# Six layer norms: four tiles' roots taken a stage earlier, turnings tile by tile, 20 unread products ahead of them

## The reference

```python
def _layernorm(x, axis=-1, eps=1e-05):
    m = jnp.mean(x, axis=axis, keepdims=True)
    v = jnp.var(x, axis=axis, keepdims=True)
    return (x - m) / jnp.sqrt(v + eps)

x = x + 0.5 * L0_ffn(_layernorm(x), ...)   # stage 0: dense 512x512 and a low-rank part mixed by 8 soft experts
x = x + L0_attn(_layernorm(x), ...)        # stage 1: causal attention, 32 heads of 16, with 10 adapter keys
x = x + 0.5 * L0_ffn(_layernorm(x), ...)   # stage 2: as stage 0
x = x + 0.5 * L1_ffn(_layernorm(x), ...)   # stage 3: 16 experts, the best 2 of each token, and a shared one
x = x + L1_attn(_layernorm(x), ...)        # stage 4: grouped attention, 32 heads of 128 on 8 keys, no mask
x = x + 0.5 * L1_ffn(_layernorm(x), ...)   # stage 5: as stage 3
```

## Time and profile before

| | |
|---|---|
| median of 3 runs | 1725.32 us (1724.57 to 1725.44) |
| profiled execution, its own time | 1734.16 us |
| its span | 1732.3 us |
| mean granted TensorE clock | 0.97 of full speed |
| busy: TensorE, VectorE, ScalarE, GpSimd | 93%, 58%, 53%, 57% of the span |
| norm instructions of the six stages (L168) start at | 11.0, 64.0, 425.8, 478.7, 677.0, 1534.3 us |

### The profile page before, as it was taken

How to read it: one execution, slowest core, us unless ns; L and a number is a source line. 1 busy time by engine, 2 the same in 40 slices (tenths; PEclk the granted TensorE clock), 3 DMA queues, 4 the chain that set the end, 5 groups by cost and what they waited for, 6 DMA issues and landing times. The chain is left out here.

```text
span 1732.3 us, 26681 instructions
## 1 busy us (share of the span) xinstructions
PE 1603.9 (93%) x8364; PEld 1248.4 (72%) x8364; DVE 1001.3 (58%) x2614; ACT 914.6 (53%) x1881; POOL 990.0 (57%) x1156
## 2 busy tenths in 40 slices
PE   6899999998979996889999999999999999979998
PEld 4587565656667874678878787877878788767886
DVE  6651656644583237465665666666675756666235
ACT  2212767661232222677777777777777777731231
POOL 2342646530313632688777788778787787812533
PEclk9899989998989998999999999999999999989999
DMA  2200000001076643445344443534445344454934
GB/s 88 104 1 3 2 1 2 2 2 38 1 271 220 226 151 115 91 104 122 86 110 111 107 115 79 124 94 109 121 100 131 73 104 91 92 184 161 344 126 152
DMA packets 311297, 179.99 MB, mean 104 GB/s; under 512 B 281608, under 2 KB 282968, under 8 KB 308769
## 3 DMA queue, kind: packets, MB, share of 16 engines
q1 hardware_dynamic: 299360, 152.54, 31.4%
q0 software_dynamic: 11840, 26.25, 4.8%
HBM read 111.08 MB, written 22.54 MB: 77 GB/s over the span
## 5 line engine op out<-in xcount | busy, mean ns | idle before, releaser
L1381 POOL TENSOR_TENSOR st_prob<-st_prob,st_rinv 128x512 f32<-128x512 f32 x256 | 273.7, 1069 | 167.4 <-DVE st_rinv L1463 167.4
L1385 POOL TENSOR_TENSOR st_plane<-st_prob,st_plane 128x512 f16<-128x512 f32 x256 | 311.1, 1226 | 0.2
L1470 DVE TENSOR_REDUCE st_nmax<-st_score 128x1 f32<-128x512 f32 x256 | 175.3, 685 | 198.1 <-PE st_score L114 197.6
L1316 ACT ACTIVATE st_prob<-st_score,st_nmax 128x512 f32<-128x512 f32 x256 | 175.3, 685 | 82.2 <-DVE st_nmax L1470 80.3
L1300 ACT ACTIVATE st_plane<-st_prob 128x512 f16<-128x512 f32 x256 | 160.3, 626 | 108.1 <-POOL st_prob L1381 107.9
L1426 DVE CAST st_ptlo<-st_plane_t 128x512 fp32r<-128x512 f16 x256 | 175.2, 685 | 2.4 <-DMA st_plane_t<-st_plane 2.4
L1295 ACT ACTIVATE st_pthi<-st_plane_t 128x512 fp32r<-128x512 f16 x256 | 159.7, 624 | 6.8 <-DMA st_plane_t<-st_plane 6.6
L2143 DVE CUSTOM_DVE_ANT_0 st1b_dump<-st1b_score,st1b_maskrow 128x128 f32<-128x128 f32 (+3 forms) x256 | 112.8, 488 | 82.2 <-PE st1b_score L1796 56.5
L791 POOL DMA_INDIRECT st_xg<-rows,st_source x62 | 62.8, 1013 | 108.3 <-DVE st_source L979 61.3
L1992 ACT ACTIVATE st1b_slabs<-st1b_across 128x512 f32<-128x512 f32 (+1 forms) x192 | 91.1, 531 | 61.0 <-PE st1b_across L1818 45.8
L661 PE MATMUL st_bank<-st_xts,st_raw 128*128 128x128 f32 x992 | 121.0, 275 | 0.7 <-issue 0.7
(11 more groups left out here) (395 smaller groups left out, 4001.4 us busy)
## 6 DMA issues: line engine op xcount, KB each, us to landing
st_raw<-in_moe_w SPq DMA_DIRECT2D x40, 768.0 KB, 17.8
sorted_outs<-st_ln_xn SPq DMA_DIRECT2D x62, 256.0 KB
st_qraw<-in_gqa_q SPq DMA_DIRECT2D x8, 1024.0 KB, 5.2
st_oraw<-in_gqa_o SPq DMA_DIRECT2D x8, 1024.0 KB, 5.2
rows<-st_ln_xn SPq DMA_DIRECT2D x2, 2048.0 KB, 14.7
st_kvraw<-in_gqa_kv SPq DMA_DIRECT2D x8, 512.0 KB, 3.9
st_plane_t<-st_plane SPq DMA_TRANSPOSE x256
st1a_raw<-in_w_attn SPq DMA_DIRECT2D x3, 1024.0 KB, 5.5
```

The lines of the kernel that those rows point to most:

```text
L1316: act.activation(prob[:, t, :], score[t][:, :], ACT.Exp, bias=nmax[:, slot:slot + 1], accum_out=rsum[:, slot:slot + 1]).then_inc(exp_ready, 1)
L1381: pool.tensor_tensor(prob[:, t, :], prob[:, t, :], rinv[:, slot:slot + 1].broadcast_to([P, T]), ALU.mult).then_inc(norm_ready, 1)
L1385: pool.tensor_tensor(plane[t][:, T:2 * T], prob[:, t, :], plane[t][:, 0:T], ALU.subtract).then_inc(lower_ready, 1)
L1470: dve.tensor_reduce(nmax[:, slot:slot + 1], score[t][:, :], AX, ALU.max, negate=True).then_inc(nmax_ready, 1)
```

## The change

- `Moments.early` on VectorE, once the statistics of four tiles are there (tiles 0 to 3): aggregation of these four, variance plus epsilon, a wait for ScalarE's root (`early_root`), and the chain of five (`inverse_root`). It stands in the stage that makes x; in stage 0's entry it stands between the fourth and the fifth tile's statistics. `close` aggregates only tiles 4 to 7.
- `vector_rows` then issues the variance of the late four tiles, the rows of the first four, and behind them the wait for the late root, the late chain and four rows.
- The turnings go tile by tile: TensorE waits for one row and turns its four blocks into four banks, so that the four banks of a half are complete with the fourth tile's turnings.
- Ahead of the turnings of each norm stand 20 products of the identity by itself, into the last bank of the norm.
- In stages 0 and 2 the statistics of the seventh tile and `early` stand ahead of the last add. In stage 3 the statistics of tiles 0 to 3 and `early` stand ahead of the four last adds. In stage 4 ScalarE's `root_table` and `early_root` stand ahead of `out_hi`.
- The small buffers of the roots are shared by all stages.

```diff
+def inverse_root(dve, root, cols, step, done):
+    ve, ra, rb, rc = (root[n][:, cols] for n in ("ve", "ra", "rb", "rc"))
+    dve.reciprocal(ra, root["sd"][:, cols]).then_inc(step, 1)
+    dve.wait_ge(step, done + 1)
+    dve.tensor_tensor(rb, ra, ra, ALU.mult).then_inc(step, 1)
+    dve.wait_ge(step, done + 2)
+    dve.tensor_tensor(rc, rb, ve, ALU.mult).then_inc(step, 1)
+    dve.wait_ge(step, done + 3)
+    dve.tensor_scalar(rb, rc, -0.5, 1.5, ALU.mult, ALU.add).then_inc(step, 1)
+    dve.wait_ge(step, done + 4)
+    dve.tensor_tensor(rc, ra, rb, ALU.mult).then_inc(step, 1)
+    dve.wait_ge(step, done + 5)
...
 class Moments:
...
+    def early(self, dve, taken):
+        half = slice(0, TB)
+        dve.wait_ge(self.stats_ready, taken)
+        for t in range(TB):
+            dve.bn_aggr(self.mv[:, t, :], self.stats[:, t, :]).then_inc(self.mv_step, 1)
+        dve.wait_ge(self.mv_step, TB)
+        dve.tensor_scalar(self.root["ve"][:, half], self.mv[:, half, 1], 1e-5, None, ALU.add).then_inc(self.mv_step, 1)
+        dve.wait_ge(self.early_std, 1)
+        inverse_root(dve, self.root, half, self.mv_step, TB + 1)
+
+    def early_root(self, act):
+        act.wait_ge(self.mv_step, TB + 1)
+        act.activation(self.root["sd"][:, 0:TB], self.root["ve"][:, 0:TB], ACT.Sqrt).then_inc(self.early_std, 1)
+
+    def close(self, dve, rest):
         dve.wait_ge(self.stats_ready, NT)
-        for t in range(NT):
-            dve.bn_aggr(self.mv[:, t, :], self.stats[:, t, :]).then_inc(self.mv_ready, 1)
-        dve.wait_ge(self.mv_ready, NT)
+        for t in rest:
+            dve.bn_aggr(self.mv[:, t, :], self.stats[:, t, :]).then_inc(self.mv_step, 1)
+        dve.wait_ge(self.mv_step, NT + 6)
...
 class Norm:
...
     def vector_rows(self, dve):
+        late = slice(self.early, NT)
+        def row(t):
+            dve.tensor_scalar(self.rows[t], self.x[:, t, :], self.mv[:, t, 0:1], self.root["rc"][:, t:t + 1],
+                              ALU.subtract, ALU.mult).then_inc(self.xn_ready, 1)
+        dve.tensor_scalar(self.root["ve"][:, late], self.mv[:, late, 1], 1e-5, None, ALU.add).then_inc(self.var_ready, 1)
+        for t in range(self.early):
+            row(t)
         dve.wait_ge(self.std_ready, 1)
...
+        inverse_root(dve, self.root, late, self.rstd_step, 0)
+        for t in range(self.early, NT):
+            row(t)
...
     def tensor(self, pe):
-        for n, (h, k) in enumerate(self.order):
-            pe.wait_ge(self.xn_ready, TB * (h + 1))
+        warm(pe, self.bank[-1], self.ident, 20)
+        for h in range(B):
             for t in range(TB):
-                last = pe.transpose(self.bank[n][:, t * P:(t + 1) * P], self.rows[h * TB + t][:, k * P:(k + 1) * P], self.ident[:, :])
-            last.then_inc(self.turned_ready, 1)
+                pe.wait_ge(self.xn_ready, TB * h + t + 1)
+                for k in range(KC):
+                    last = pe.transpose(self.bank[h * KC + k][:, t * P:(t + 1) * P], self.rows[h * TB + t][:, k * P:(k + 1) * P], self.ident[:, :])
+                    if t == TB - 1:
+                        last.then_inc(self.turned_ready, 1)
...
# stage 0, ScalarE
                     entry.root_table(act)
+                    entry.early_root(act)
                 norm.scalar_std(act)
...
# stage 0, VectorE
                         entry.take(dve, t)
-                    entry.close(dve)
+                        if t == TB - 1:
+                            entry.early(dve, TB)
+                    entry.close(dve, range(TB, NT))
...
# stages 0 and 2, VectorE, ahead of the adds
                 for j in range(NT):
+                    if j == NT - 1:
+                        dve.wait_ge(x_added, j)
+                        moments.take(dve, order[j - 1])
+                        moments.early(dve, j)
                     dve.wait_ge(tile_ready, j + 1)
...
-                    if j >= 1:
+                    if 1 <= j < NT - 1:
...
# stages 3 and 5, VectorE
-                for t in range(TB):
-                    add_step(NI - 1, 1)
+                if not last_stage:
+                    for t in range(TB):
+                        wait(dve, *written[t])
+                        moments.take(dve, t)
+                    moments.early(dve, TB)
+                add_step(NI - 1, 1)
+                for t in range(TB, NT):
+                    if t + 1 < NT:
+                        add_step(NI - 1, 1)
                     if not last_stage:
                         wait(dve, *written[t])
                         moments.take(dve, t)
...
# stage 4, ScalarE
                     turned_hi(LAST, NU - 1, t)
+                moments.root_table(act)
+                moments.early_root(act)
                 out_hi(LAST, NU - 1)
-                moments.root_table(act)
...
# stages 1 and 4, VectorE, behind the statistics of tiles 0 to 3
+                moments.early(dve, TB)
```

More of the change, by code:

```diff
@@ L1018, in _ @@
                 if not last_stage:
[L1019 to L1022 removed]
+                    moments.close(dve, range(TB, NT))
 def gqa_stage(nc, env, dram, name):
```

50 lines of the change are left out of this document (20 added, 30 removed).

## The result

| | before | after |
|---|---|---|
| time, median of 8 runs (lowest to highest) | 1725.32 us (1714.22 to 1728.27) | 1736.09 us (1734.81 to 1746.19) |
| ratio, with its 95% interval | | 1.0081 (1.0057 to 1.0105) |
| the profiled execution: time, span | 1734.16, 1732.3 us | 1746.19, 1744.5 us |
| TensorE busy, records | 1603.9 us, 8364 | 1629.8 us, 8604 |
| mean granted clock | 0.970 | 0.975 |

The change makes the kernel 0.8% slower, 14 us by the ratio; the two medians lie 10.8 us apart. More runs on another chip gave 1.0074 (1.0053 to 1.0096). The forecast was 7.8 us slower. The sign was right, the size was about half of the ratio's; the measured 1736.1 lies inside the range given, 3 us above the point.

The account below looks back on a forecast made before the run. TensorE, busy 93%, bounds the kernel, so only moves of each norm's gate (a stage's first product waiting for four xlo) and of stage ends count; terms sum to +7.8 us, forecast 1733.1, range 1726.5 to 1739.

Parts of the forecast that it names:

- stage 2: Second FFN stage's norm: products begin where turnings stood, less 0.3 us each for start and rows; gate +2.3 us.
- rival 2: All norms: fast clock comes 6.4 us after the start, products take 7.5 us; some +14 us, 1739; chance 0.10.
- The price of 20 products: Head of each norm: 40 records, partly at 1.2 GHz, together 6.8 us.
- Rival 3: All norms: an identity product takes one pass, head 4.3 us; sum +1.2 us, 1726.5; chance 0.03.
- rival 1: All norms: products meet or quickly make 2.4 GHz, 4.6 us instead of 6.8; sum -0.4, 1724.9; chance 0.13.
- Stage 0: Entry norm: a VectorE row held by GpSimd's wlo, gate +3.1 us, 0.9 back from the clock; +2.2 us.
- Rival 4: Stage 0: VectorE isn't held, roots pay; last row at 20; with rival 1 some -4 us, 1721.5; chance 0.06.
- Stage 1: Heads stage's norm: gate waits for GpSimd's wlo, -0.2 us, and warmer clock behind it gives 1.3; -1.5 us.
- End of the first expert stage: Last adds wait behind four statistics and the early part; +0.6 or, at low clock, +3.1 us; taken as +2.1.
- Stage 3: First expert stage's norm: gate 11.45 us after TensorE's start, at 489.9 instead of 488.19; +1.7 us.
- Stages 4 and 5: Norms of grouped attention and last stage: 11.45 us from start to gate; +0.6 and +0.4 us.
- The first bank: Each norm: first bank is full only with the fourth tile's first turning, 13 records, 1.45 us.

Follow-up runs that it names:

- forty products: Changed kernel with 40 identity products at each norm in place of 20; ratio 1.0266 to the kernel before.
- old entry and tail: Changed kernel with one root for eight tiles in stage 0 and the first expert stage's last adds in front, as before; ratio 1.0086 to the kernel before.
- bank by bank: Changed kernel with the turnings ordered as before, four of one bank and then the next bank; ratio 1.0068 to the kernel before.
- all but the products undone: Changed kernel with old stage 0 and expert-end orders, turnings by bank, 40 filling instructions; products and other early roots stay; ratio 1.0043 to the kernel before.
- no products: Changed kernel without the 20 products at each norm, all else kept; ratio 1.0054 to the kernel before.

## Why the prediction was right in sign and half in size

Two steps failed. One is in the sum: "TensorE reaches the products where the turnings stood, less 0.3 each" gave stage 2 +2.3 us, and it measured +4.3, because the chain that lets TensorE go on had not moved. The other is a term that the prediction put at nothing: "Behind it TensorE runs nearly without gaps, so I price each norm by how far its gate moves". Behind the gate of the grouped attention five instructions more in ScalarE's program made five stalls, 3.6 us. The rest of the difference is sizes. That the time lies inside the range is partly luck, since the range's upper end belongs to rival 2, and 7.5 us of products at every norm is not what came.

The terms of the sum, in its order, against what the two profiles of the changed kernel show beside those of the kernel before:

- **The price of 20 products.** Right. 40 records each, 6.97, 6.33, 7.23, 6.41, 7.54 and 6.72 us; their mean is 6.87, the forecast had 6.8. (One record is 0.117 us at 2.4 GHz, by forty against twenty, not 0.115; the row read for it, 2.47 us for 20 records, holds the end of the last one too.) They have one spread from stage to stage, as the low clock takes more or less of each. Rival 3 (one pass) and rival 1 (4.6 us) are out for these two profiles, and so is rival 2's 7.5 everywhere.
- **Stage 0**, +2.2: gate +3.2 and +2.7 in the two profiles (forecast +3.1), and 1.2 us back behind it from the clock (0.9): +1.7. The held row is the mechanism that was named; wlo began at 17.35, not 17.5. Rival 4 is out. With the old entry the gate was at 24.7, so the early root costs 1.5 of it.
- **Stage 1**, -1.5: -1.7, of which 0.1 at the gate and 1.6 behind it, where no matmul was slow.
- **Stage 2**, +2.3: +4.4 and +4.5 at the gate, less 0.15 behind it: +4.3. The step that failed is "TensorE reaches the products where the turnings stood, less 0.3 each". What TensorE waited for there was neither rows nor the stage's start but the chain load, low-rank product, aw copy (the row says so: the head waits 0.28 us for `st_aw`), and that chain had not moved. And the clock was low until 439.2, not for 3 us of the head: 7.23 us and not 6.0. By the terms: start 0.6, head 1.2, turning to copy 0.2.
- **End of the first expert stage**, +2.1: +3.1 and +3.0. The mechanism and both ends of the range were right, and it was the end with the low clock; I had rounded a three in four down. Against all seventeen profiles it is +2.5, nearer to the forecast.
- **Stage 3**, +1.7: +1.6.
- **Stages 4 and 5**, +0.6 and +0.4: +1.3 and +0.7 against the first profile, but against six more executions in which these norms were as before (11.2 to 11.8, mean 11.4, and 11.2 to 12.2, mean 11.6, from end to gate) more like +2.2 and +1.4. The profile on which the sum was made had late gates there by itself; I took one execution's 10.83 for the price of the stage. The head of stage 4 was 7.54 us.
- **The first bank**, 1.45 us in the sum, took 1.62 us every time. Small, but bank by bank it takes 0.64; that tile by tile costs 1 us at each gate behind products was inside the sum and nowhere named.
- **Not in the sum at all**: the stalls of ScalarE's loop in the attention, 3.6 us at +5 instructions without the change, and what the same body lost with it (851.9 and 850.8 against 845.2 and 848.1, 847.4 with the loop moved on by 40). I had priced every instruction that ScalarE got, in place, and none by where it puts those behind it.

Taken together: +1.7 - 1.7 + 4.3 + 3.05 + 1.6 + 1.3 + 0.7 + 3.6 = +14.6 us, beside 14 (9.8 to 18.1) measured. The forecast's 7.8, the 3.6 of the stalls, 2.0 more in stage 2, 0.95 at the expert end and 1.0 in stages 4 and 5, less 0.8 in stages 0, 1 and 3, are the same sum. With the terms from more executions (2.5 at the expert end, 2.2 and 1.4 in stages 4 and 5) it is 15.6. So the agreement to half a microsecond is luck, that within the interval isn't. The spans of the two first profiles themselves differ by 12.2 us, and chance is in that too: the first expert stage took 173.8 us from its gate to the last combining against 177.7 before, and the last stage 181.7 from its gate against 187.3; in the second pair of profiles these were 177.3 against 177.0 and 188.3 against 185.8. What makes them so was not looked for. The full price of twenty products is read from forty against twenty, 28 us; the first twenty cost less, since a part of them stood beside rows, loads and splits.

What stays open: the rest of the attention's difference. In three profiles (the changed kernel twice, and with 40 instructions of filling) TensorE lost 1.4 to 1.7 us more at a wait for a pthi copy some 130 us behind the gate; in the other fourteen, forty products among them, it did not. And three ratios (old entry and tail, all but the products, no products) are 3 to 8 us above what the gates, ends and stalls of their traces give.

## What to carry to other kernels

Work put in front of a gate to warm a clock is paid in full unless a named wait at that gate ends later than the work does: here one gate of six had such a wait (a GpSimd split behind a load), and there it gave back 1.6 us in the trace, which the time didn't show (0.9994). When an edit lengthens an engine's program ahead of a loop, compare the idle time "issue" and the count of instruction packets inside that loop before and after; a loop of 279 instructions began to be fetched anew at each jump back when it lay 2 to 18 instructions further on, and at 30 and more it had stopped. Price an order of "statistics first, adds second" by who waits for the adds, and take a stage's base from more than one execution.

## What the runs showed of the hardware that was not expected

- ScalarE stalls 1.4 to 2.7 us at a jump back in a band of positions of its loop: bad at 2, 4, 5 and 18 instructions from the kernel before, good at 0, 30, 44 and 45, with five more 8 KB packets a pass where it stalls. Seven profiles with five stalls lost 2.6 to 3.7 us by them.
- The low clock of the heads stage differs between executions of one kernel (24 and 31 us before, 31 and 21 after), and it moves that stage by more than any term of the change: the same 2240 matmuls took 343.6 to 355.3 us. These are the windows from gate to end for the kernel before and for all but the products undone (PE busy, PEld, DVE, ACT, POOL, then the clock, DMA share and GB/s):

```profile
76.08:425.28 349.20, 333.06 (x2240) 227.28 (x2240) 184.97 (x664) 172.55 (x347) 156.75 (x413) 0.97 0.02 8
```

```profile
74.76:418.37 343.61, 327.69 (x2240) 223.28 (x2240) 186.56 (x671) 173.21 (x348) 156.25 (x413) 0.99 0.02 8
```

- A row of VectorE stood through a GpSimd subtraction whenever rows were left when it began (6.08 us for four rows here, 8.24 for eight with the old entry). One execution, of the kernel before with 30 idle instructions, shows what that is worth. The load of w came 2 us late, so wlo began only when the rows were done:

```profile
13.34 4.05 DVE L181 TENSOR_SCALAR st_ln_xn<-all_x,all_mv,st_ln_rc 128x512 f32<-128x512 f32 x8
14.70 0.31 ACT L339 ACTIVATE st_aw<-st_w 128x128 f32<-128x128 f32 x1 [1.36 <-DMA st_w<-in_w]
17.41 4.60 POOL L363 TENSOR_TENSOR st_wlo<-st_w,st_whi 128x2048 fp32r<-128x2048 f32 x1 [1.21 <-DVE st_ln_xn L181]
20.47 0.40 PE L112 MATMUL st_bank<-all_xhi,st_awhi 128*48 128x512 f32 x1
```

  Everything started 0.8 us later than in the earlier trace rows, and the gate came 2.8 us earlier, at 20.47. A late load helped. Holding wlo back on purpose until the last row was not tried.
